# Window attention on one core: row maxima turned by VectorE in blocks of 32 and sent as four partial rows

## The reference

```python
def _L0_attn_ref(x, w_qkv):                      # H = 16 heads, window W = 128, E = 32
    q, k, v = jnp.split(x @ w_qkv, 3, axis=-1)   # to windows: (B, H, nw, W, E)
    # keys and values of the window before, the window itself and the one behind it
    scores = jnp.einsum('bhnqe,bhnke->bhnqk', q * scale, k_ctx)
    scores = jnp.where(valid, scores, NEG)
    attn = softmax(scores)
    out = jnp.einsum('bhnqk,bhnke->bhnqe', attn, v_ctx)
...
x = x + layernorm(_L0_attn_ref(layernorm(x), w_qkv))
x = x + layernorm(_L0_ffn_ref(layernorm(x), ...))   # a mixture of expert weights per batch entry
```

## Time and profile before

| what | us |
|---|---|
| median of 3 runs | 2935.64 (2930.39 to 2939.09) |
| the profiled execution | 2937.19 |
| its span, first to last instruction | 2935.3 |
| PE busy | 2867.0 (98%) |
| DVE busy | 1994.9 (68%) |
| ACT busy | 1727.5 (59%) |
| POOL busy | 853.4 (29%) |

### The profile page before, as it was taken

One profiled execution on the slowest core, in us unless ns is written; L12 is line 12 of the kernel. 1 busy time (PEld: TensorE's weight loads), 2 busy tenths in 40 slices (PEclk: granted clock), 3 DMA queues, 4 the chain that ended last, 5 costly groups with the idle time before them and its releaser, 6 DMA issues.

```text
span 2935.3 us, 55438 instructions
## 1 busy us (share of the span) xinstructions
PE 2867.0 (98%) x20252; PEld 2378.8 (81%) x20252; DVE 1994.9 (68%) x3769; ACT 1727.5 (59%) x3385; POOL 853.4 (29%) x713
## 2 busy tenths in 40 slices
PE   8999999999999999989989999999999999999998
PEld 6888888788888887778767888788888888888886
DVE  5333333488888887888868766886768766796664
ACT  3222222377767776665636666866667666676666
POOL 1000000188888887974400000500005000040003
PEclk9999999999999999999989999999999999999999
DMA  6555555678788889959999866985769765895642
GB/s 215 184 174 171 183 186 194 221 191 199 196 198 199 198 201 216 227 180 399 389 394 333 286 208 207 354 319 200 254 212 404 265 205 199 289 399 196 232 137 86
DMA packets 361429, 697.10 MB, mean 237 GB/s; under 512 B 26576, under 2 KB 127056, under 8 KB 361184
## 3 DMA queue, kind: packets, MB, share of 16 engines
q1 hardware_dynamic: 335456, 629.63, 67.0%
q10 hardware_dynamic: 17424, 32.24, 3.1%
q0 software_dynamic: 8304, 31.98, 2.7%
HBM read 525.45 MB, written 167.78 MB: 236 GB/s over the span
## 4 chain that ended last, share of the span: by engine, by line
PE 83%; DMA 6%; DVE 4%; issue 3%; ACT 2%; POOL 2%; ACTq 0%; DVEq 0%; SPq 0%; POOLq 0%
PE a_acc L571 18%; PE e_acc L1407 7%; PE e_hid L1390 7%; PE e_hid L1391 7%; PE e_hid L1392 7%; PE e_acc L1409 7%; PE e_acc L1408 7%; PE a_ps_score L622 5%; PE a_ps_keys L641 5%; PE a_ps_out L670 5%; DMA a_q_st<-a_max_rows 3%; DMA a_gate_att<-o_scratch 3%; PE a_ps_out L678 2%; PE a_ps_turn L688 1%; POOL a_gate_x L1231 1%
## 5 line engine op out<-in xcount | busy, mean ns | idle before, releaser
L1780 DVE SCALAR_TENSOR_TENSOR e_part<-e_ring,e_g_cols,e_part 128x512 f32<-128x512 f32 x896 | 647.5, 778 | 5.7 <-DMA e_ring<-mix_rows 3.2
L487 DVE TENSOR_REDUCE a_neg_max<-a_ps_score 128x1 f32<-128x384 f32 (+1 forms) x1024 | 490.1, 526 | 48.8 <-PE a_ps_score L622 47.5
L323 POOL TENSOR_TENSOR a_total<-a_probs 128x512 f32<-128x512 f32 x256 | 323.8, 1281 | 591.5 <-ACT a_probs L415 591.2
L415 ACT ACTIVATE a_probs<-a_ps_keys 128x384 f32<-128x384 f32 (+1 forms) x1024 | 422.8, 477 | 46.3 <-PE a_ps_keys L641 22.8
L1804 DVE TENSOR_TENSOR e_u_lo<-e_u,e_u_hi 128x512 fp32r<-128x512 f32 x256 | 180.0, 703 | 372.8 <-ACT e_u_hi L1538 372.6
L1534 ACT ACTIVATE e_u<-e_hid,e_mb 128x512 f32<-128x512 f32 x256 | 176.9, 691 | 432.0 <-PE e_hid L1392 419.4
L1263 POOL TENSOR_SCALAR e_var<-e_moments 128x4 f32<-128x4 f32 x15 | 6.7, 445 | 1273.4 <-DVE e_moments L1816 1272.7
L622 PE MATMUL a_ps_score<-a_k_st,a_q_st 96*128 96x384 f32 (+1 forms) x1024 | 332.5, 359 | 3.7 <-DMA a_q_st<-qk_scratch 2.8
L641 PE MATMUL a_ps_keys<-a_q_st,a_k_st 97*128 97x384 f32 (+1 forms) x1024 | 318.8, 353 | 12.3 <-DMA a_q_st<-a_max_rows 11.2
L333 POOL TENSOR_TENSOR a_total<-a_total,a_probs 128x512 f32<-128x512 f32 x224 | 286.3, 1281 | 58.0 <-ACT a_probs L415 55.5
L467 DVE TENSOR_TENSOR a_qk<-a_acc,a_qk 128x512 fp32r<-128x512 f32 x128 | 88.1, 690 | 308.1 <-ACT a_qk L364 308.1
(11 more groups left out here) (154 smaller groups left out, 6465.8 us busy)
## 6 DMA issues: line engine op xcount, KB each, us to landing
e_ring<-mix_rows SPq DMA_DIRECT2D x558, 512.0 KB, 5.5
qk_scratch<-a_qk SPq DMA_DIRECT2D x128, 512.0 KB, 3.3
a_k_st<-qk_scratch SPq DMA_DIRECT2D x180, 256.0 KB, 4.4
a_q_st<-qk_scratch SPq DMA_DIRECT2D x180, 256.0 KB, 4.4
v_scratch<-a_v SPq DMA_DIRECT2D x64, 256.0 KB, 3.1
a_v_sb<-v_scratch SPq DMA_DIRECT2D x64, 256.0 KB, 5.0
o_scratch<-a_out SPq DMA_DIRECT2D x128, 128.0 KB, 3.1
x_scratch<-a_gate_x POOLq DMA_DIRECT2D x16, 1024.0 KB, 10.2
```

The costliest lines, as they stand in the source:

```text
L323: add = pool.tensor_tensor(total[:, g % 2, i], p[0], p[1], ALU.add)
L415: act.activation(probs[:, m % PROBS, h, 0:(hi - lo) * WIN], ps_keys[x % TRIO][:, 0:(hi - lo) * WIN], ACT.Exp, scale=SCALE).then_inc(exp_do ...
L487: dve.tensor_reduce(neg_max[:, g % 2, i, h:h + 1], ps_score[y % TRIO][:, 0:(hi - lo) * WIN], AX_X, ALU.max, negate=True).then_inc(reduced, 1)
L1780: dve.scalar_tensor_tensor(out=part[:, n % 2, half, :], in0=ring[:, slot, :], scalar=g_cols[:, b, e:e + 1], in1=so_far, op0=ALU.mult, op1= ...
```

## The change

PE's transpose of the maxima, its PSUM rows and DVE's copy of them go. Instead DVE does two instructions after reduce 0 of each step. The first (`tensor_tensor`, MULT) writes spread, 128 x (4 blocks x 32): for each block b of 32 columns the 8 maxima of the partition, times own_block, which is 1 where the partition belongs to block b and 0 elsewhere. (The columns within a block are h x 8 + i, and those of i = 2 to 7 stay zero.) The second (`transpose`) turns each 32 x 32 block of the 128 x 128 numbers for itself into max_rows. A maximum row now lies on four partitions, one for each block of 32 queries, each with zeros outside its own block. The two DMAs of a step each carry 16 partitions of max_rows (4 blocks x 4 heads) to rows 96 to 99 of q_st, and k_st has ones in rows 96 to 99: the keys product sums the four rows. It has 100 rows for 97.

Both DMAs of a step are now issued by ACT, between exp 2 and copy_out. SP issues only those of the first two steps. `rows_landed` has one semaphore for both windows of a step, so keys product 4 of a step waits until both rows of the next step's maxima have landed, where it waited for the first one. `turn_out` has no wait for rows_done any more. POOL sets spread to zero and own_block, once, and puts ones in four rows of k_st instead of one.

```diff
-        def send_row(eng, g, i):
-            w = 2 * (g % HALF) + i
+        def send_rows(eng, g):
             eng.wait_ge(rows_done, g + 1)
-            eng.dma_start(q_st[STACK:STACK + 1, :, w * WIN:(w + 1) * WIN].bitcast(F32),
-                          max_rows[QH * i:QH * (i + 1), g % 2, :].bitcast(F32)).then_inc(rows_landed[i][g % 2], 16)
+            for i in range(2):
+                w = 2 * (g % HALF) + i
+                eng.dma_start(q_st[STACK:STACK + P // E, :, w * WIN:(w + 1) * WIN].bitcast(F32),
+                              max_rows[i:P:E // QH, g % 2, :].bitcast(F32)).then_inc(rows_landed[g % 2], 16)
...
+            pool.memset(spread[:, :, :].bitcast(F32), 0.0).then_inc(const_done, 1)
...
-            pool.memset(k_st[STACK:STACK + 1, :, :].bitcast(F32), 1.0).then_inc(const_done, 1)
+            pool.memset(k_st[STACK:STACK + P // E, :, :].bitcast(F32), 1.0).then_inc(const_done, 1)
...
+                if there(T + AHEAD - 1):
+                    send_rows(act, T + AHEAD - 1)
                 if there(T - LAG):
                     copy_out(T - LAG)
                 for x in range(3, UNITS):
                     if there(T):
                         weights(T, x)
-                    if x == 4 and there(T + AHEAD - 1):
-                        send_row(act, T + AHEAD - 1, 0)
...
-            def copy_rows(g):
+            def turn_max(g):
+                dve.wait_ge(reduced, UNITS * (g + 1))
+                if g >= 1:
+                    dve.wait_ge(rows_done, g)
+                dve.tensor_tensor(spread[:, :, :].rearrange("p b (h i) -> p b i h", h=QH)[:, :, 0:2],
+                                  neg_max[:, g % 2].unsqueeze(1).to_broadcast([P, P // E, 2, QH]),
+                                  own_block[:, :].unsqueeze(2).unsqueeze(3).to_broadcast([P, P // E, 2, QH]),
+                                  ALU.mult).then_inc(spread_done, 1)
+                dve.wait_ge(spread_done, g + 1)
                 if g >= 2:
-                    for i in range(2):
-                        dve.wait_ge(rows_landed[i][g % 2], 16 * (g // 2))
-                dve.wait_ge(max_turned, g + 1)
-                dve.tensor_copy(max_rows[:, g % 2, :], ps_turn[0:2 * QH, 0, :]).then_inc(rows_done, 1)
+                    dve.wait_ge(rows_landed[g % 2], 32 * (g // 2))
+                dve.transpose(max_rows[:, g % 2, :].bitcast(F32), spread[:, :, :].bitcast(F32).rearrange("p b c -> p (b c)")).then_inc(rows_done, 1)
```

More of the change, by code:

```diff
@@ L73, in attention_programs @@
         neg_max = sb("neg_max", [P, 2, 2, QH], F32)
+        spread = sb("spread", [P, P // E, E], F32R)
+        own_block = sb("own_block", [P, P // E], F32)
         inv_sum = sb("inv_sum", [P, 2, 2, QH], F32)
         ones = sb("ones", [P, 2, E], F32)
-        max_rows = sb("max_rows", [2 * QH, 2, WIN], F32R)
+        max_rows = sb("max_rows", [P, 2, WIN], F32R)
         q_st = sb("q_st", [P, QH, SEQ], F32R)
@@ L148, in attention_programs @@
         reduced = sem("reduced")
-        max_turned = sem("max_turned")
+        spread_done = sem("spread_done")
         rows_done = sem("rows_done")
-        rows_landed = [[sem(f"rows_landed{i}{p}") for p in range(2)] for i in range(2)]
+        rows_landed = [sem(f"rows_landed{p}") for p in range(2)]
         keys_done = sem("keys_done")
@@ L254, in sync @@
                 if g == 5:
-                    for i in range(2):
-                        send_row(sp, 0, i)
-            for i in range(2):
-                send_row(sp, 1, i)
+                    send_rows(sp, 0)
+            send_rows(sp, 1)
             store_v(PAIRS - 1, 1)
@@ L306, in gpsimd @@
                 pool.wait_ge(const_done, 2 + i)
+            pool.wait_ge(const_done, 3)
+            pool.memset(spread[:, :, :].bitcast(F32), 0.0).then_inc(const_done, 1)
+            pool.wait_ge(const_done, 4)
+            pool.memset(own_block[:, :], 0.0).then_inc(const_done, 1)
+            for b in range(P // E):
+                pool.wait_ge(const_done, 5 + b)
+                pool.memset(own_block[b * E:(b + 1) * E, b:b + 1], 1.0).then_inc(const_done, 1)
+            pool.wait_ge(const_done, 9)
             pool.wait_ge(xn_done, 1)
-            pool.memset(k_st[STACK:STACK + 1, :, :].bitcast(F32), 1.0).then_inc(const_done, 1)
+            pool.memset(k_st[STACK:STACK + P // E, :, :].bitcast(F32), 1.0).then_inc(const_done, 1)
             def parts(m):
@@ L540, in vector @@
                 if g == 5:
-                    copy_rows(0)
+                    turn_max(0)
                 if g == 9:
-                    copy_rows(1)
+                    turn_max(1)
             for T in range(STEPS + LAG):
                 if there(T + AHEAD):
-                    for s in range(3):
-                        reduce(T + AHEAD, s)
+                    reduce(T + AHEAD, 0)
                 if there(T + AHEAD - 1):
-                    copy_rows(T + AHEAD - 1)
+                    turn_max(T + AHEAD - 1)
                 if there(T + AHEAD):
-                    for s in range(3, UNITS):
+                    for s in range(1, UNITS):
                         reduce(T + AHEAD, s)
@@ L640, in keys @@
                     pe.wait_ge(v_done, TILES * CHUNKS + x + 1)
[L641 to L648, removed]
-                pe.transpose(ps_turn[0:2 * QH, 0, :], neg_max[:, g % 2].rearrange("p w h -> p (w h)"), ident[:, :])\
-                  .then_inc(max_turned, 1)
+                pe.matmul(ps_keys[x % TRIO][:, 0:(hi - lo) * WIN], k_st[0:STACK + P // E, h, w * WIN:(w + 1) * WIN],
+                          q_st[0:STACK + P // E, h, lo * WIN:hi * WIN], start=True, stop=True).then_inc(keys_done, 1)
             def values(g):
@@ L742, in tensor @@
                 along(T)
-                if there(T + AHEAD - 1):
-                    turn_max(T + AHEAD - 1)
                 scores(T, [3])
```

19 lines of the change are left out of this document (5 added, 14 removed).

## The result

The changed kernel takes 3021.99 us (median; 3017.14 to 3022.46), the kernel before 2935.43 in the same comparison: a ratio of 1.0288, interval 1.0274 to 1.0302. It is 86.6 us slower. The forecast was 2991, in a range of 2925 to 3055, with 0.80 on slower. The sign and the mechanism held; the size was 31 us short, of +56 forecast.

What follows compares the result with a forecast made beforehand. ACT's chain from copy_out to the next burst was taken to have no slack, beside a busy PE. +59 for ordinary steps, +7 for the last 25 and -10 for rows made +56: 2991 us, range 2925 to 3055.

Steps and rivals of the forecast that it cites:

- The hold: DVE's product behind reduction 0, both inputs in SBUF, waits 0.86 us for POOL's addition to end and ends 0.04 later.
- The transpose: DVE's new transpose behind the product takes 0.28 us, between 0.16 and 0.49.
- Case (D): Rival: DVE's transpose waits for POOL too, 1.25 us and more in each step, about +260 us, 3195; chance 0.04.
- The delay in a late step: ACT waits for the maxima, then issues two DMAs: copy_out 0.93 us late (0.81 to 1.14), the burst with it.
- How many steps: Between one step in two and every step is late, since a late step gives DVE time; two thirds taken.
- case (A): Rival: late in every step, 125 x 0.93 - 10 = +106, 3042 us; chance 0.20.
- What PE gives back: Without the maxima's transpose PE gains 0.03 to 0.22 us a step, 0.1 taken, only while ACT isn't late.
- The sum: 0.59 us more a step: +59 for about 100 ordinary steps, +7 for the last 25, -10 for rows: +56.
- rows that land sooner: Keys products waited 15.9 us for rows not landed; with earlier issue 10 us (0 to 16) come back.
- the last steps: The last 25 steps carry gate work and are longer for other reasons, which hide about half: +7.
- (B): Rival: POOL doesn't hold the product up; steps keep 5.42 us, the 10 us for rows are gained, 2926 us; chance 0.10.
- (C): Rival: product always meets the border, ACT never late, PE gets its full 0.22 us a step, 2896 us; chance 0.06.

Runs made afterwards that it cites:

- unread product: Kernel before, plus on DVE behind reduction 0 of each step a 32-element product of two SBUF inputs that nobody reads: 2959.22 us, ratio 1.0093.
- the mask in PSUM: Changed kernel, with own_block copied once to a free row of ps_turn in PSUM and read there by the product: 2945.78 us, ratio 1.0040 to the kernel before.
- the kernel with two semaphores: Changed kernel with own_block in PSUM, one row DMA on ACT ahead of copy_out, one on SP, rows_landed separate for each window: 2921.56 us, ratio 0.9948.
- A second transpose: Kernel before, with PE's transpose of the maxima done twice in each step, one behind the other: 2942.68 us, ratio 1.0027.
- the kernel with one issue each: Changed kernel with own_block in PSUM, one row DMA issued by ACT ahead of copy_out, the other by SP, rows_landed still merged: 2937.55 us, ratio 1.0009.
- two issues among the exps: Changed kernel with both DMAs issued behind exp 4: 2995.23 us (1.0223) with the product's inputs in SBUF, 2993.06 (1.0207) with own_block in PSUM.

## Why the prediction was right, and where it was not

**The hold.** Right, in kind and size. 0.86 us of waiting plus 0.04 was forecast; the late step shows 1.19 in place of 0.20. It ends with POOL's addition in the changed kernel and in the kernel before with an unread product, and is gone with the mask in PSUM. The rule of the Trainium skill that the forecast cited for it ("SBUF — State Buffer", Who interferes with whom) speaks of two SBUF inputs: the 197/204/211 ns with one of them in PSUM agree with it. That the later instruction waits only until the earlier one ends holds for most products here and not for all: two of the 128 were held for 3.42 and 4.24 us, through more than one of POOL's instructions.

**The transpose.** Estimated at 0.28 us between 0.16 and 0.49, measured 0.311. The figure that the forecast cited from the Trainium skill ("VectorE: DVE Perf Modes", The three transpose paths), 311 ns, was for bf16; the same holds here for fp32. Case (D), a transpose that also waits for POOL, falls: 311/311/314 ns in all 128, with POOL's next addition running beside it (from 1072.52, the transpose from 1072.68).

**The delay in a late step.** copy_out 1.31 us late was measured, 0.93 forecast. By the late step whose burst starts at 1070.92: the border that lets the product in lies 1.60 us into the burst, not 1.42 (+0.18); the product ends 0.12 behind it, not 0.04 (+0.08); transpose, issues and the gaps between them take 1.62 to copy_out's start, not 1.50 (+0.12, of which the transpose is 0.03 and the issues none: 1.14 for two). Against it stands 0.31 that the forecast left out: from copy_out to the next burst there are 3.08 us (1074.26 to 1077.34) instead of 3.39. Two things give it back. No issue stands among the exps: the kernel with two semaphores, which has none there either and copy_out on time, needs 3.28. The other 0.20 comes from the lateness itself, because a late copy_out finds the keys products done: exp 3 starts 0.39 us behind it and not 0.53. Keys product 3 before (copy_out at 1020.32) and in the late step (copy_out at 1074.26):

```profile
1020.47 0.34 PE L641 MATMUL a_ps_keys<-a_q_st,a_k_st 97*128 97x384 f32 x1
...
1073.09 0.34 PE L652 MATMUL a_ps_keys<-a_q_st,a_k_st 100*128 100x384 f32 x1
```

So it isn't quite true that whatever delays copy_out delays the burst by as much. The net of 1.0 a step is near 0.93, with two errors that nearly cancel.

**How many steps. This step failed, though its number came out near.** I took two thirds and it is five eighths. My reason was that a late step gives DVE time, so that the next product comes 0.16 us into the burst and meets a border there with 0.05 us to spare. Nothing of that happens. In every late step up to the gate work the product starts 0.53 us into the burst, because DVE can't use the time: reduction 7 waits 0.60 us for score 7 (1076.36), and score 7 hangs on exp 3 through keys 6, just as the burst does. The forecast had reduction 7 end 0.84 us ahead of the next burst (1023.8 for 1024.64); it ends 0.42 ahead of it (1076.92 for 1077.34), and these 0.4 us are what put the product behind the border. PE's part of this, and DVE's reduction 7:

```profile
1075.19 0.45 PE L652 MATMUL a_ps_keys<-a_q_st,a_k_st 100*128 100x384 f32 x1 [0.33 <-ACT a_probs L422]
1075.47 0.49 PE L690 MATMUL a_ps_turn<-ident,a_out_t 128*128 128x128 f32 x3
1075.72 0.42 PE L652 MATMUL a_ps_keys<-a_q_st,a_k_st 100*128 100x384 f32 x1
1075.98 0.52 PE L635 MATMUL a_ps_score<-a_k_st,a_q_st 96*128 96x384 f32 x2
...
1076.36 0.56 DVE L494 TENSOR_REDUCE a_neg_max<-a_ps_score 128x1 f32<-128x384 f32 x1 [0.60 <-PE a_ps_score L635]
```

Keys 6, the three transposes of the output, keys 7, score 7: whatever moves exp 3 moves score 7 and the burst alike, and the product's place in the burst doesn't change. What does change from step to step is POOL, which has gaps and fewer additions at a sequence's ends, and the reduction, which is shorter for edge windows. The three of eight that escape are of that sort: one reduction of 0.41 us, and two steps at a sequence's end where the product started in a gap or right ahead of a border (1102.15 in a gap from 1102.13, 1107.48 just ahead of a border near 1107.60). I had listed this as a point against case (A); it was the whole answer. That two thirds came so near was luck.

**What PE gives back.** Forecast 0.1 between 0.03 and 0.22 us. A second transpose costs 0.07 to 0.10. But that one more costs this doesn't show that taking one away gives it back. The kernel with two semaphores has 0.13 less at the median of its steps (5.21 against 5.34), and there the issue has left the exps as well. Its copy_out stands where it stood, 2.02 us into the burst, and exp 3, the first whose keys product stands behind the burst, starts 0.52 us behind it instead of 0.53: so far PE's transpose gave back 0.01. Exp 5 starts 1.28 us behind copy_out instead of 1.52, and the next burst 3.28 instead of 3.40 (medians of steps with full windows). So nearly all of the 0.13 is more likely the issue's, and no run shows the 0.1 of the forecast. In the changed kernel little shows either, even in the steps that aren't held (5.31 against 5.35).

**The sum.** By stages, from burst starts in the two traces:

| stretch | before | after | difference | forecast |
|---|---|---|---|---|
| start to the first burst | 581.8 | 584.4 | +2.6 | 0 |
| bursts 1 to 97 | 516.5 | 576.0 | +59.5 | +59 |
| bursts 97 to 128 | 186.5 | 205.7 | +19.2 | +7 |
| rest | 1650.5 | 1654.6 | +4.1 | 0 |
| rows that land sooner | | | in the above | -10 |

The main term held. **Two terms were mis-sized.** In the last steps I let gate work hide half; it hides nothing there in the sum: 0.62 us for each of the 31, as in the others. The two products of 3.42 and 4.24 us stand there too, in steps of 9.77 and 11.72 us, and a hold of more than one addition was in no term. And the rows: their waits fell from 15.9 to 11.4 us, 4.5 and not 10, and merging the two semaphores works against it, as the kernel with one issue each showed. The +2.6 and +4.1 outside I can't explain. The last stretch had between 1649.9 and 1656.7 in the traces of all kernels, without an order that I can see, so part of it may be noise. Of the 29 us between the forecast +56 and the +85 of the traces, 12 are the last steps, 10 the rows and 7 the stretches outside.

**The parts together**, by the ratios: with one issue on each queue, two semaphores and the mask in PSUM the change is worth -0.5%. Both issues on ACT ahead of copy_out, with the one semaphore, take that to +0.4%. The mask in SBUF takes it to +2.9%. Of the other cases, (B) is what the kernel became with the mask in PSUM, though at 2946 and not 2926. Its ordinary steps kept their length, as (B) says; but the 10 us for the rows didn't come as time, though the waits for rows fell to 6.2 us, and the last steps and the rest took 9 us more. (C) asked for maxima within 0.86 us of the burst's start; with the mask in PSUM they come at 1.07 (1034.41 for 1033.34), so the gain needed one issue fewer on ACT. (A) falls with the three steps in eight. 

## What to carry to other kernels

Before a small operation goes from TensorE to VectorE, look at what POOL runs at that moment and where the operands lie: here a product of 32 elements waited until POOL's running addition of 1.25 us was over when both its inputs were in SBUF (1.17 us in the median), and for nothing when one was in PSUM (0.20). Ask next who waits for the result: the same hold cost about 75 us with ACT's chain behind it, 18 to 26 with VectorE alone late, and nothing measurable where two issues among the exps made ACT's chain the longest. And where a delay seems to repair itself in the next step, check that the engine which should catch up isn't fed by the one that is late.

## What the runs showed of the hardware that I had not expected

A held VectorE instruction can miss borders. Most get in at the first, but in the kernel with the unread product one stood through four of them (DVE, then POOL):

```profile
1209.77 6.07 DVE L558 TENSOR_TENSOR a_spread<-a_ones,a_own_block 128x32 f32<-128x32 f32 x1
...
1209.62 2.52 POOL L328 TENSOR_TENSOR a_total<-a_probs 128x512 f32<-128x512 f32 x2
1212.08 2.50 POOL L338 TENSOR_TENSOR a_total<-a_total,a_probs 128x512 f32<-128x512 f32 x2
1214.52 1.28 POOL L1243 TENSOR_TENSOR a_gate_x<-a_gate_x,a_gate_x_in 128x512 f32<-128x512 f32 x1
```

It ends at 1215.84, with the last of five POOL instructions that follow each other without a gap (1215.79). In the changed kernel two of 128 took more than one addition, 4.24 us the longer one. What decides who gets in at a border no run here shows.

A DMA issue takes ACT's queue 0.55 to 0.58 us in the median wherever it stands, but its price differs: nothing in the idle time ahead of copy_out, where one fits; 0.24 us at the next exp for one among them (exp 5 starts 1.52 us behind copy_out, and 1.28 in the kernel with two semaphores, where there is none), of which 0.12 reach the burst; and two among them lengthened the median step by 0.55 us (5.89 against 5.34, where one already stood).

PE's transpose of 8 columns is recorded with 0.27 us, and one more of them costs 0.07 to 0.10 us of time.
